# Attention of a fused decoder layer: context tiles first, causal mask after the exponential, softmax sums inverted as 32x128 and spread through DRAM

## The reference

```python
x = x + mamba(layernorm(x))                      # state space scan, 512 channels, 16 states
x = x + cross_attention(layernorm(x), ctx_512)   # 16 heads of 16
x = x + ffn(layernorm(x))                        # dense branch and 8 experts, top 2

def cross_attention(x, c):
    q, k, v = heads(x @ Wq + bq), heads(x @ Wk + bk), heads(x @ Wv + bv)
    y = softmax(causal(q @ k.T / 4)) @ v
    qc, kc, vc = heads(x @ Wcq + bcq), heads(c @ Wck + bck), heads(c @ Wcv + bcv)
    y = y + softmax(qc @ kc.T / 4) @ vc
    return y @ Wp + bp
```

## Time and profile before

| | us |
|---|---|
| median of 3 runs (2007.1 to 2014.9) | 2013.3 |
| profiled execution, its own time | 2016.2 |
| profiled execution, span | 2014.4 |
| PE busy | 1555.1 (77%) |
| DVE busy | 1374.3 (68%) |
| ACT busy | 834.3 (41%) |
| POOL busy | 654.8 (33%) |

### The profile page before, as it was taken

How to read it: one execution, slowest core, us unless ns; L and a number is a source line. 1 busy time by engine, 2 the same in 40 slices (tenths; PEclk the granted TensorE clock), 3 DMA queues, 4 the chain that set the end, 5 groups by cost and what they waited for, 6 DMA issues and landing times. The chain is left out here.

```text
span 2014.4 us, 19539 instructions
## 1 busy us (share of the span) xinstructions
PE 1555.1 (77%) x6696; PEld 750.1 (37%) x6696; DVE 1374.3 (68%) x2056; ACT 834.3 (41%) x1570; POOL 654.8 (33%) x423
## 2 busy tenths in 40 slices
PE   5796789884986789874977798855557898669985
PEld 2353322231553322242544222222233222348874
DVE  5997577648995767468986777389966765333334
ACT  4541346655441255645432366643313456322211
POOL 2664401222863401125653211227644021112221
PEclk9898789996997899987998799978988899779998
DMA  5910621003000630002003510021006210227754
GB/s 162 345 55 0 154 64 41 1 0 116 17 0 23 162 73 3 1 31 99 3 0 88 130 40 1 1 84 44 0 0 157 48 33 1 64 98 245 232 179 127
DMA packets 123491, 147.44 MB, mean 73 GB/s; under 512 B 18117, under 2 KB 106190, under 8 KB 121344
## 3 DMA queue, kind: packets, MB, share of 16 engines
q1 hardware_dynamic: 119648, 137.53, 24.4%
q0 software_dynamic: 3744, 8.66, 1.2%
HBM read 96.79 MB, written 50.79 MB: 73 GB/s over the span
## 5 line engine op out<-in xcount | busy, mean ns | idle before, releaser
L168 PE MATMUL PS<-arena 128*32 128x512 f32 (+10 forms) x4150 | 885.4, 457 | 124.4 <-ACT arena L1734 31.6
L168 PEld LDWEIGHTS PS<-arena 128*32 128x32 f32 (+3 forms) x4150 | 372.8, 128 | 615.0 <-ACT arena L1734 274.3
L1734 ACT ACTIVATE arena<-PS 128x512 f32<-128x512 f32 (+3 forms) x768 | 375.7, 541 | 321.1 <-PE PS L168 319.4
L1347 POOL TENSOR_TENSOR arena<-arena 128x1024 f32<-128x1024 f32 x128 | 305.1, 2384 | 235.8 <-DVE arena L1373 140.8
L1777 DVE TENSOR_REDUCE maxs<-PS 128x1 f32<-128x1024 f32 x256 | 303.9, 1219 | 82.8 <-PE PS L168 82.3
L1373 DVE TENSOR_TENSOR_SCAN arena<-PS,arena 128x1024 f32<-128x1024 f32 x128 | 292.2, 2283 | 6.1 <-ACT PS L1322 6.1
L168 PE MATMUL PS<-arena,ident 128*128 128x512 f32 (+1 forms) x560 | 261.7, 594 | 5.4 <-DVE arena L1382 5.4
L1322 ACT ACTIVATE PS<-arena,A_neg 128x511 f32<-128x511 f32 x256 | 165.9, 681 | 232.0 <-DVE arena L1373 183.9
L1503 POOL TENSOR_TENSOR arena<-xn 128x512 f32<-128x512 f32 x16 | 20.2, 1265 | 530.4 <-ACT xn L1723 530.4
L1382 DVE TENSOR_TENSOR arena<-arena,PS 128x1024 f32<-128x1024 f32 x128 | 156.3, 1221 | 7.7 <-PE PS L168 3.7
L1781 DVE TENSOR_REDUCE maxs<-PS 128x1 f32<-128x512 f32 (+3 forms) x256 | 108.5, 484 | 61.5 <-PE PS L168 60.8
(11 more groups left out here) (260 smaller groups left out, 1751.2 us busy)
## 6 DMA issues: line engine op xcount, KB each, us to landing
arena<-in_ew SPq DMA_DIRECT2D x46, 512.0 KB, 4.8
arena<-stack_parts SPq DMA_DIRECT2D x288, 64.0 KB, 2.4
rows_in<-nil SPq DMA_DIRECT2D x16, 1088.0 KB, 12.5
arena<-b_rows SPq DMA_DIRECT2D x16, 1024.0 KB, 7.6
stack_parts<-arena SPq DMA_DIRECT2D x40, 384.0 KB, 3.1
arena<-stack_parts SPq DMA_DIRECT2D x96, 128.0 KB, 4.5
arena<-rows_in SPq DMA_DIRECT2D x23, 272.0 KB, 5.1
arena<-picked_rows SPq DMA_DIRECT2D x16, 256.0 KB, 3.7
```

What stands on the lines that cost most here:

```text
L168: return nc.tensor.matmul(o, l, r, start=start, stop=stop)
L1347: nc.gpsimd.tensor_tensor(b_sb[i % 2], u[:, 2 * kh:2 * kh + 2, :], Brow[:, n, :].unsqueeze(1).to_broadcast([P, 2, T]), ALU.mult).then_inc( ...
L1734: nc.scalar.activation(probs[(HG * s + h) % NPR][:, 0:N], bank(4 + n % 2)[:, 0:N], ACT.Exp, scale=HD ** -0.5).then_inc(S["ring_read"], 1)
```

## The change

1. **Context first.** `TILES` begins with the two ck tiles of heads 0 to 7. Their matmuls stand at the end of `scan`, into banks 0 and 1. The eight context value tiles come before the transposes. ACT copies all value tiles; the value biases are no longer added there but multiplied with `wp` once, for b = 0, and added to `bp`. SP loads KC of group 0 first, and issues all loads of group 1 behind the causal max rows of group 0. POOL fills only the padding of V and VC, and `ones_rows(0)` waits for `xn_ready`.
2. **Mask.** The mask matmul of a causal score is gone; POOL zeroes the masked part of the 128x128 block after the exponential (16 `affine_select` a group), and `values` waits for that.
3. **Sums.** For groups 0 to 2 SP gathers the eight rows of sums as `den_c` (32x128), DVE inverts them, SP writes them to `dens` in DRAM and reads them back over all partitions; POOL does two products and a sum. The inversion stands behind 16 of the 24 reductions, before it stood behind 12. The last group is turned on PE into bank 5 (128x32), inverted from there, copied wide and spread on PE.
4. **Turns.** `JOBS_AT` gives the max jobs of each step; the causal maxima are turned between the two pairs of scores instead of behind `values`.

```diff
+    dens = nc.dram_tensor("dens", (2, HG, T), F32).ap()
...
+        den_c = sb("den_c", [2 * HG * TT, P])
+        den_t = sb("den_t", [P, 2 * TT * HG])
+        den_wide = xn[:].rearrange("p (i a) n -> p i (a n)", i=2)
...
-        TILES = [(x, hh, half) for hh in range(2) for x, half in ((0, 0), (1, 0), (2, 0), (3, 0), (3, 1))]
+        TILES = [(x, 0, half) for x, half in ((3, 0), (3, 1), (0, 0), (1, 0), (2, 0))]
+        TILES += [(x, 1, half) for x, half in ((0, 0), (1, 0), (2, 0), (3, 0), (3, 1))]
...
+                def turned_sums():
+                    pe.wait_ge(S["pv_copied"], 2 * NG)
+                    for i, y in enumerate((Y1, Y2)):
+                        for t in range(TT):
+                            last = mm(bank(5)[:, (i * TT + t) * HG:(i * TT + t + 1) * HG], y[:, tok(t)],
+                                      den_sel[:, 0:P:32], i + t == 0, i + t == TT)
+                    last.then_inc(S["turned_mm"], 1)
+
+                def spread_sums():
+                    pe.wait_ge(S["den_ready"], NG)
+                    for i in range(2):
+                        for t in range(TT):
+                            last = mm(bank(6 + i)[:, tok(t)], den_wide[:, i, tok(t)],
+                                      ident[:], True, True)
+                    last.then_inc(S["turned_mm"], 1)
...
+                def last_sums():
+                    dve.wait_ge(S["turned_mm"], 1)
+                    fed(nc.vector.reciprocal(den_t[:], bank(5)[:, 0:2 * TT * HG]))
+                    dve.wait_ge(S["y_ready"], NG - 1)
+                    nc.vector.tensor_copy(den_wide.rearrange("p i (c n) -> p (i c) n", n=32),
+                                          den_t[:].unsqueeze(2).to_broadcast([P, 2 * TT * HG, 32]))\
+                        .then_inc(S["den_ready"], 1)
+
+                def last_heads():
+                    dve.wait_ge(S["turned_mm"], 2)
+                    fed(nc.vector.tensor_tensor(Y1, Y1, bank(6), ALU.mult))
+                    fed(nc.vector.tensor_tensor(Y2, Y2, bank(7), ALU.mult))
+                    nc.vector.tensor_tensor(YT[NG - 1], Y1, Y2, ALU.add).then_inc(S["y_ready"], 1)
...
+                pe.wait_ge(S["h_done"], len(UNITS) - 1)
+                pe.wait_ge(ctx_loaded, 16 * (b + 1))
+                if b == 0:
+                    pe.wait_ge(load_later, 16 * (len(LATER) + NG * HG + 2 * HG))
+                for i in range(2):
+                    mm(bank(i), wck[:, 0:P], ctxT[:, i * T:(i + 1) * T], True, True)
...
-            FIRST_TILES = 6
+            CK_TILES, FIRST_TILES = 2, 6
+            TILE_BANKS = (0, 1, 6, 7, 4, 5, 6, 7, 6, 7)
+            VALUE_ORDER = list(range(TT, 3 * TT)) + list(range(TT))
...
                 store(0)
                 store(1)
+                stored(0)
+                stored(1)
+                load_heads(0, 3)
+                store(2)
+                store(3)
                 sp.wait_ge(S["outproj_mm"], TT)
-                stored(0)
+                stored(2)
                 load_heads(0, 0)
-                store(2)
-                stored(1)
+                store(4)
+                stored(3)
                 load_heads(0, 1)
-                store(3)
-                store(4)
-                stored(2)
+                stored(4)
                 load_heads(0, 2)
-                stored(3)
-                stored(4)
-                load_heads(0, 3)
-                store(5)
-                load_heads(1, 0)
-                load_heads(1, 1)
-                for i in range(6, len(TILES)):
+                for i in range(FIRST_TILES - 1, len(TILES)):
+                    if i == len(TILES) - 1:
+                        load_max_rows(0, CAUSAL)
                     store(i)
-                    if i == 8:
-                        load_max_rows(0, CAUSAL)
-                load_heads(1, 2)
-                load_heads(1, 3)
+                for x in range(4):
+                    load_heads(1, x)
...
+                for g in range(NG - 1):
+                    sp.wait_ge(S["pv_copied"], 2 * (g + 1))
+                    for i, y in enumerate((Y1, Y2)):
+                        sp.dma_start(den_c[i * HG * TT:(i + 1) * HG * TT, :], y[HD:P:32, :])\
+                            .then_inc(S["dens_out"], 16)
+                    if g == 0:
+                        for x in range(4):
+                            load_heads(3, x)
+                    sp.wait_ge(S["den_ready"], g + 1)
+                    sp.dma_start(dens.rearrange("i h (q p) -> (i h q) p", p=P), den_c[:]).then_inc(S["dens_kept"], 16)
+                    sp.wait_ge(S["dens_kept"], 16 * (g + 1))
+                    for i in range(2):
+                        sp.dma_start(den_sb[:, i, :], dens[i].unsqueeze(1).to_broadcast([HG, 32, T]))\
+                            .then_inc(S["dens_in"], 16)
+                    if g + 2 < NG:
+                        load_max_rows(g + 2, CAUSAL)
+                        load_max_rows(g + 2, CONTEXT)
...
+                def masks(g, k):
+                    for h in range(HG):
+                        pool.wait_ge(S["ring_read"], ring(g, k, h) + 1)
+                        own = probs[(HG * (STEPS * g + k) + h) % NPR][:, 0:P]
+                        nc.gpsimd.affine_select(out=own, in_=own, compare_op=ALU.is_ge, fill=0.0, base=0,
+                                                pattern=[[1, P]], channel_multiplier=-1).then_inc(S["masked"], 1)
...
+                link = chain(pool, S["pool_chain4"])
+                for i in range(CK_TILES):
+                    low(i)
+                pool.wait_ge(S["xn_ready"], TT)
+                pool.wait_ge(S["parts_ready"], CK_TILES)
+                pool.wait_ge(S["v_init"], 1)
                 ones_rows(0)
                 pool.wait_ge(S["ones_ready"], 2)
-                for i in range(len(TILES)):
-                    pool.wait_ge(S["mid_ready"], i + 1)
-                    nc.gpsimd.tensor_tensor(pt[i % NPT][:, 2, :], r_sb[i % 2], pt[i % NPT][:, 1, :], ALU.subtract)\
-                        .then_inc(S["parts_ready"], 1)
-                pool.wait_ge(S["xn_ready"], TT)
-                link = chain(pool, S["pool_chain4"])
+                for i in range(CK_TILES, len(TILES)):
+                    low(i)
+                for k in range(TT):
+                    masks(0, k)
+                if b == 0:
+                    pool.wait_ge(S["bp_ready"], 1)
                 link(nc.gpsimd.tensor_tensor(x1[:], x1[:], bp[:].unsqueeze(1).to_broadcast([P, TT, DM]), ALU.add))
-                pool.wait_ge(S["parts_ready"], len(TILES))
+                pool.wait_ge(S["masked"], HG * TT)
                 ones_rows(1)
                 all_stored(pool)
                 ones_rows(2)
                 pool.wait_ge(S["ones_ready"], 2 * NPAR)
-                for g in range(NG):
-                    pool.wait_ge(S["ring_read"], ring_den(g, 1) + 1)
-                    nc.gpsimd.tensor_tensor(R1, den_sb[:, 0, :], den_sb[:, 1, :], ALU.mult)\
-                        .then_inc(S["den_ready"], 1)
-                    nc.gpsimd.tensor_tensor(Y1, Y1, den_sb[:, 1, :], ALU.mult)
-                    link(nc.gpsimd.tensor_tensor(Y2, Y2, den_sb[:, 0, :], ALU.mult))
-                    link(nc.gpsimd.tensor_tensor(Y1, Y1, Y2, ALU.add))
-                    pool.wait_ge(S["norm_ready"], g + 1)
-                    nc.gpsimd.tensor_tensor(YT[g], Y1, R2, ALU.mult).then_inc(S["y_ready"], 1)
+                for g in range(NG - 1):
+                    for k in range(TT):
+                        masks(g + 1, k)
+                    pool.wait_ge(S["dens_in"], 2 * 16 * (g + 1))
+                    nc.gpsimd.tensor_tensor(Y1, Y1, den_sb[:, 0, :], ALU.mult)
+                    link(nc.gpsimd.tensor_tensor(Y2, Y2, den_sb[:, 1, :], ALU.mult))
+                    nc.gpsimd.tensor_tensor(YT[g], Y1, Y2, ALU.add).then_inc(S["y_ready"], 1)
...
+                for j in range(2 * TT):
+                    value_tile(j)
+                if b == 0:
+                    pe.wait_ge(S["rest_ready"], CK_TILES)
+                    for i in range(2 * NG):
+                        last = mm(bank(0)[:, 0:DM], v_bias[:, i // NG, i % NG].unsqueeze(1).to_broadcast([P, P]),
+                                  wp[:, i % NG, :], i == 0, i == 2 * NG - 1)
+                    last.then_inc(S["bp_mm"], 1)
+                    pe.wait_ge(S["bp_ready"], 1)
+                pe.wait_ge(S["rest_ready"], CK_TILES)
...
-                            mm(o[:, 0:T - k * P], K[par][0:SR, h, tok(k)], Q[par][0:SR, h, k * P:T],
-                               True, False)
-                            last = mm(o[:, 0:P], identb[:], mask_kq[:], False, True)
+                            last = mm(o[:, 0:T - k * P], K[par][0:SR, h, tok(k)], Q[par][0:SR, h, k * P:T],
+                                      True, True)
                         last.then_inc(S["ring_mm"], 1)
 
-                def denominators(g):
-                    pe.wait_ge(S["pv_copied"], 2 * (g + 1))
```

(32 more changed lines are left out.)

195 lines of the change are left out of this document (81 added, 114 removed).

## The result

The changed kernel takes 1991.2 us (median of 4 runs, 1989.6 to 1994.8) against 2014.1 for the kernel before beside it (2007.1 to 2015.9): ratio 0.9895, 95% interval 0.9868 to 0.9923. It is faster by about 1% (23 us), and the interval excludes 1. The prediction was 1930 us with 1900 to 1975, so 61 us of the 84 expected are missing and the time lies outside the range. The profiled execution has a span of 1990.0 us, against 2014.4.

A forecast was written before the change was run, and what follows sets the result against it. PE's order of work bounds group 1; earlier attention waits for rows and DMAs. 21.9 us a sequence, times four 87.6, less 3.5 and 5.1, plus 4.0: 83.0 off 2016.2 gives 1933, forecast 1930, range 1900 to 1975.

The forecast's parts named there:

- the new wait of groups 1 and 2: At the causal copy, ACT waits 4.2 us for the inverted sums; 3.5 us lost in each of two groups.
- broadcast read of 256 KB about 3.0: In the inverted sums' round trip through DRAM, the read back takes about 3.0 us, bounds 1.6 and 3.7.
- 2.3 lost: Before group 0's context rows, PE runs causal max jobs at half clock for 4.5 us: 2.3 lost, bounds 0 and 5.
- the round trip is longer: Rival: 2 us more on two hops of the sums' DRAM trip, stall 7.5 instead of 3.5, time 1962; 15%.
- The prediction's own sign of being wrong: Attention stages of b = 1 and 2 shorter by under 12 or over 28 us would show it wrong.
- From the projection to the context rows of group 0: Start of each sequence's attention: 13.8 us gained, 10.3 in b = 0, where the bias work stands.
- that rival: Start of attention: the xT copy waits for two POOL memsets, xT 4.4 us later four times, time 1948; 5%.
- the slower rival: Causal steps bound by POOL's masks: at 1.27 us each a step takes 5.1 instead of 2.54, time 2093; 6%.
- Groups 1 and 2 without the stall: Masks, sums and causal turns gain 5.5 us in group 1 and 4.8 in group 2, before the wait is subtracted.
- Group 3: Last group of each sequence: gains 2.3 + 1.0 = 3.3 us, with no wait since DVE inverts at once.
- The entries: End of attention in entries 1 to 3: in_w starts about 1.7 us later behind the sums' turning and spreading on PE.
- The last entry: Final output projection: chain 1.3 us shorter and gaps small enough for full clock, 4.0 us saved once.

The follow-up runs named there:

- the kernel without the stall: Changed kernel with the inversion behind 8 reductions instead of 16 and the broadcast read cut by heads, outermost dimension 32: 1914.7 us, ratio 0.9499.

## Why the prediction was wrong

**The step that failed** is the new wait of groups 1 and 2: "`y_ready` comes at t8 + 9.8 ... It stands 4.2 us ... 3.5 lost". Its mechanism was right, in place (inversion at the start of step 8, ACT ahead of `copy_causal` behind step 9, not in group 3) and in kind. One term of its sum was too small, and one was put at nothing:

- "broadcast read of 256 KB about 3.0", with bounds 1.6 and 3.7 from rows of other shapes. With the issue it was 7.7 to 7.9 us instead of 3.5, above both bounds. The experiments with 2 and 32 in place of 4 show that the outermost dimension decides it. So the wait is 8.4 instead of 4.2. The two reads share this rate: an estimate from the 97 GB/s above gives 2.7 us for the data of the second one, which the prediction had counted only as an issue of 0.5.
- The clock. "About 0.7 us is slack" was right, as the waits of 0.9 to 1.9 us show. But behind a wait of this length PE runs at half clock, and that adds 1.7 us. The prediction reckoned with such a fall in group 0 (2.3 lost) and had no term for it here.

Together: 3.5 forecast, 4.2 by the longer wait and 1.7 by the clock make 9.4. By the changed kernel (groups 1 and 2 together 382.7 us over four sequences) and by the kernel without the stall (307.6) the stall costs 75.1 us, where the prediction had 28. The rival "the round trip is longer" named this place and asked for 2 us more on two hops; 4.2 came on one.

Over the whole table 83.0 us were forecast and 19.6 found. Of the 63 that are missing the stall has 47, group 3 has 6.7, the last entry 4.6, groups 1 and 2 without the stall 4.4 and the other entries 2.4; up to the copy of group 0 some 2 us more were gained than forecast. The prediction's own sign of being wrong came: the attention stages of b = 1 and 2, from the projection to the copy of group 3, are 11 and 8 us shorter, under its 12. Two slips in the working are small: 9.8 less 5.4 is 4.4 and not 4.2, and the 2.3 of group 3 has no working. The 2.0 us that it cites from the Trainium skill stand in a section on DMAs that GpSimd issues; here SP issues them.

**Right.** From the projection to the context rows of group 0: 15.8, 13.1 and 12.9 us in b = 1 to 3, and 10.9 in b = 0, against 13.8 and 10.3. The DVE instruction takes 0.17 us, the xT copy beside a memset 0.69 (that rival falls). The out projection takes 8.8, 7.2, 7.1 and 8.8 us instead of 9.9, 9.9, 8.8 and 8.7, which is 1.3 less on average, as forecast. PE waits 4.20 us ahead of the first max job and 0.8 to 1.25 for DVE at the context jobs, for no DMA. The mask on POOL takes 0.30 us and hides (the slower rival falls). Group 0's context part gains 2.9, 1.6, 0.8 and 1.5; without the cast beside a memset each would be 1.3 more (an estimate from 1.51 and 0.21).

**Groups 1 and 2 without the stall.** Forecast 5.5 and 4.8; found 36.8 over four sequences, 4.6 each on average against 5.15. Inside this the mask was worth 0.4 and not 1.0, and the turns 1.4 and 1.7 and not 1.7 and 1.0. The errors went both ways and the sum nearly held, which is partly luck.

**Group 3.** 3.3 forecast; 2.7 and 3.7 in b = 1 and 2, but 0.6 and -0.5 in b = 0 and 3, where the window is 33.3 us at a clock of 0.85 against 30.3 at 1.00. That is 6.7 us of the missing; what sets the clock there is open.

**The entries.** 1.7 later was forecast, 2.5 found: the transposes take 1.95 us there, not 1, and the spreading 2.6, not 1.8. No run took these apart.

**The last entry.** "Its gaps small enough for full clock, 4.0 saved" was wrong: 0.6 lost. With PE's gaps of 1.25 and 2.23 us the clock was 0.50 in the spreading and 0.71 in the projection, which took 9.99 us, about as before (9.76). With the gaps filled that stretch takes 15.5 us instead of 20.2.

## What to carry to other kernels

Price a DMA that is waited for by the outermost dimension of its access patterns as well as by its bytes; a broadcast written with few rows outermost runs on few engines, and more DMAs of the same kind do not help. Put a chain of small steps whose answer is due late (sums, inversion, round trip, spreading) as early in its engines' orders as its inputs allow, and look in the issuing queue for what stands between its links: moving one instruction on DVE and 24 loads on SP was worth 77 us here, more than three times the whole change. When a wait is priced, add what PE loses at half clock behind it: nothing for waits up to 1.9 us here, 1.4 to 1.7 from 2.7 us on. Where PE waits and runs at half clock behind it, work without use in the gap can pay. And when memsets move to a new place on POOL, look at what DVE does there: here they left one DVE instruction (3.43 us) and came to stand beside another (1.51).

## What the runs showed of the hardware that was not expected

- The same 512 KB of broadcast in packets of 2 KB took 13.6, 7.7 and 4.5 us with outermost dimension 2, 4 and 32, the first and the last with four DMAs and the second with two. While the data flowed the share of the 16 DMA engines was 0.15, 0.27 and 0.71.
- Waits of 0.9 to 1.9 us of ACT cost a group 0.7 us less than their length, at a clock of 1.00; waits of 2.7 to 9.0 us cost 0.6 to 1.1 more than their length, at 0.96 to 0.89.
- Matmuls without use made the kernel 21 us faster (1909.8 to 1888.7) and the last entry 3.2 us shorter (18.7 to 15.5). In the windows shown the granted clock was at its upper level where it had been at its lower one.
- A DVE instruction on 128x4 int32 took 3.43 us beside a memset on POOL of 3.54 and 0.17 without; the two f32 instructions just ahead of it ended with the shorter memset before (at 626.9 in b = 1), after 0.52 and 0.45 instead of 0.17 and 0.16; a cast of 16x128 took 1.51 beside a memset of 1.80 and 0.21 without; a copy of 128x512 out of PSUM kept its 0.69.
- A write of 16 KB that lands in 1.4 us by itself needed 4.9 behind 24 loads of heads in the same queue.
